# The outer product in every pair of steps from the second chunk on, and a new order of TensorE's work within a pair

## The chip, the cores and the metric

The kernel runs on one core of one Trainium2 chip. The metric is the device time of one execution in microseconds. Engines are named as the profile names them: PE is TensorE (PEld its weight loads), DVE VectorE, ACT ScalarE, POOL GpSimd, SP SyncE. ACTq and SPq are the sequencers of ACT and SP issuing DMAs.

## What is computed

A selective state space layer (two batches, 1024 steps, 512 channels, 128 states) is followed by a feed-forward layer of hidden width 2048, both with a residual and a layer norm. The recurrence is sequential in the steps and is the heart of the kernel:

```python
def step(h, inp):
    dt, bt, ct, xt = inp
    h = jnp.exp(dt[:, :, None] * A) * h + (dt * xt)[:, :, None] * bt[:, None, :]
    y = jnp.einsum('bdn,bn->bd', h, ct)
    return (h, y)
```

Its inputs come from projections of the normed input (a mask by a sigmoid, `x_proj`, softplus of `dt_proj`). Its output goes through `out_proj`, the layer norm, a gate and an up projection with silu, a down projection, and the second layer norm.

## The kernel before

**Tiling.** The 1024 steps are 8 chunks of 128 steps. The state of one batch is a tile of 128 states by 512 channels, in a ring `h` of seven steps. VectorE walks through the steps in pairs (t, t+1) with t even. For each step and batch it makes a `product` (L774, the decay `a` times the state before) and a `total` (L796, the product plus the step's input, which is `u_bc` or `v_bc` scaled by a column of `BCt`). A plain pair is eight such instructions.

**The outer product.** In a pair that is in `on_x`, the input of step t for batch 1 is not added by VectorE. TensorE adds it in PSUM instead: `add_inputs` (L1418) multiplies nine bf16 rows of `x_row` and accumulates into `m_ps[:, 1, :]`, on top of the product of (t, batch 1). VectorE's product of (t+1, batch 1), which is the one that writes `m_sb`, then reads that bank and waits for TensorE. ScalarE copies the bank into `h` (`state`, L1137), which is what the product of (t+2, batch 1) has to wait for, since it writes over the bank. Such a pair is seven VectorE instructions. The same copy must be there before `y_row` of step t.

**Who is in `on_x`.** `LOAD` gives the ScalarE time of each stage of side work in tenths of a microsecond. A running sum of it, less `X_BUDGET` (20) for each pair, must be zero. That holds for 378 of the 448 pairs from the second chunk on. The other 70 stand where softplus (`soft`), the layer norms (`ln1`, `ln2`) or squares (`sq`) fall.

**The other work of a pair.** The decays of the steps ahead are made in units q, one for each pair: POOL lays out `dexp` (L661), TensorE multiplies it with A (`exponents`, L1348, 16 matmuls of 32 rows into four banks), ScalarE takes the exponential into `a` (its `exponents`, L1120). TensorE's `exponents(q)` waits for ScalarE's of q-1, and ScalarE's for TensorE's of q. A row of the output is made from `h` and `cz` by `y_row` (L1435). All else is side work: a stage is placed by `timetable` in one of four slots of a pair (two for each step) and is carried out by TensorE and ScalarE (and POOL, for the pieces) when their loops come to that slot. All side work of TensorE goes through one PSUM bank, `work`, so that a stage waits until ScalarE has emptied it: the gate and up products `gu` (L1182, two halves for each block) are emptied by `act` (L1085 to L1089), the products `down` (L1324) by `dnc`, `outp` by `ln1`.

**The order in a pair.** Each engine carries out its instructions strictly in the order of its own loop over steps and slots. TensorE before: y rows of the two steps before, side work of slot 0, the outer product, side work of slot 1, exponents, side work of slots 2 and 3. ScalarE before: exponents, side work of slots 0, 1 and 2, `state`, side work of slot 3.

**Where it is set.** `P_AT` and `EXP_AT` map a slot to the unit q whose matmuls (TensorE) and exponential (ScalarE) are done there; slot 2t is the first slot of step t.

Of the kernel before, what the change touches and what calls it, by code (L numbers as in the profile page):

```python
# [21 lines left out]
TILES_P = KB // PAIR * BLOCKS  # L22
# [11 lines left out]
ROW = D + N  # L34
X_RING = 8
X_AHEAD = 4
X_BUDGET = 20
Z_AHEAD = 4
E_RING = 4
CZ_RING = 3  # L40
# [14 lines left out]
def exp_slot(q):  # L55


    return max(4 * q - 8 * (A_RING - 1), 2 * (q - 2))


USED_UP = {SEQ - 7: (0,), SEQ - 3: (1,)}
EXP_AT = {exp_slot(q): q for q in range(2, TILES_P)}
P_AT = {exp_slot(q) - (2 if exp_slot(q) > 2 * (q - 2) else 0): q for q in range(2, TILES_P)}
DEXP_AHEAD = 6


# [136 lines left out]
def build(nc, xT, x_rows, vecs, d_param, sel_wT, xproj_wT, dt_wT, out_wT, A_log, gu_w, down_w, out_rows):  # L203
# [5 lines left out]
    with ctx:  # L209
# [187 lines left out]
        def at_steps(t, steps):  # L397

            return [(stage, j) for step in range(max(t, 0), t + steps) for slot in (SLOTS * (step % TB), SLOTS * (step % TB) + 1)
                    for stage, _, j in plans[step // TB].get(slot, ())]  # L400
# [8 lines left out]
        on_x, busy = {}, 0  # L409
        for t in range(FIRST_X, SEQ, 2):  # L410
            busy = max(0, busy + sum(LOAD.get(stage, 0) for stage, _ in at_steps(t, 2)) - X_BUDGET)
            if not busy:
# [22 lines left out]
        def row_of(k):  # L435

            first = k % G * GP
            return x_row[first:first + RANK, k % X_RING // G, :]
# [398 lines left out]
        def scalar(e):  # L837
# [276 lines left out]
            def exponents(q, src):  # L1114
                blk = q // 2
                e.wait_ge(s_p, q + 1)
                if blk >= A_RING:
                    e.wait_ge(s_m, BATCH * BS * (blk - A_RING + 1))
                dst = a[:, blk % A_RING, :, :, q % 2 * PAIR * P:(q % 2 + 1) * PAIR * P]
                e.activation(dst.rearrange("p b t (x j) -> p x (b t) j", j=GP),  # L1120
                             src.rearrange("p g (i r j) -> p (g i) r j", i=PAIR, j=GP), ACT.Exp, scale=-1.0).then_inc(s_exp, 1)
# [26 lines left out]
            for t in range(SEQ):  # L1148
# [10 lines left out]
                for i in range(SLOTS):  # L1159
                    if SLOTS * t + i in EXP_AT:  # L1160
                        exponents(EXP_AT[SLOTS * t + i], p_ps)

# [16 lines left out]
        def tensor(e):  # L1179
# [159 lines left out]
            def exponents(q, dst):  # L1339

                if q:
                    e.wait_ge(s_exp, q)
                e.wait_ge(s_dexp, q + 1)
                for i in range(PAIR):
                    for g in range(G):
                        rows = slice(g * GP, (g + 1) * GP)
                        lays = dexp[rows, q % E_RING, BATCH * i:BATCH * (i + 1), :, :].rearrange("p b t j -> p (b t j)")
                        last = e.matmul(dst[:, g, i * COLS:(i + 1) * COLS], A[rows, q % 2 * PAIR + i, :], lays, start=True,  # L1348
                                        stop=True)
                last.then_inc(s_p, 1)  # L1350
# [61 lines left out]
            def add_inputs(t):  # L1412

                k = on_x[t]
                row = row_of(k)
                e.wait_ge(d_row[k % X_RING], 16 * (k // X_RING + 1))
                e.wait_ge(s_m, BATCH * (t + 1))
                e.matmul(m_ps[:, 1, :], row[:, D:], row[:, 0:D], start=False, stop=True, skip_group_check=True  # L1418
                         ).then_inc(s_acc, 1)

            def y_row(t):
                blk, i = t // CS, t % WIN // 2
                if t == 0:
                    e.wait_ge(s_ucp, BATCH * FIRST_U)
                elif t % WIN == 0:
                    e.wait_ge(s_ycp, t // WIN)
                e.wait_ge(s_cz, blk + 1)
                e.wait_ge(s_h, sums_before(t + 1))
                if t in on_x:
                    e.wait_ge(s_hx, on_x[t] + 1)  # L1430
                for b in range(BATCH):
                    entry = (blk % CZ_RING * BATCH + b) * CS + t % CS
                    first = GP * entry + GP - 1 - i
                    group = 2 * (t % 2) + b
                    last = e.matmul(y_ps[group * GP:(group + 1) * GP, :], cz[:, first:first + GP],  # L1435
                                    h[:, t % H_RING, b * D:(b + 1) * D], start=i == 0, stop=i == GP - 1)
                last.then_inc(s_y, 1)

            first_chunk()
            for t in range(SEQ):  # L1440
                c = t // TB
                for i in range(SLOTS):
                    if SLOTS * t + i in P_AT:
                        exponents(P_AT[SLOTS * t + i], p_ps)
                    if i == 0 and t % 2 == 0 and t:
                        y_row(t - 2)
                        y_row(t - 1)
                    if i and t in on_x:
                        add_inputs(t)
                    for stage, x, j in plans[c].get(SLOTS * (t % TB) + i, ()):  # L1450
                        behind(x, stage, j)
                        before(x, stage, j)
# [10 lines left out]
        block.vector(vector)  # L1463
        block.gpsimd(gpsimd)
        block.tensor(tensor)

# [41 lines left out]
```

## Time and profile before

| | us |
|---|---|
| Median of 3 runs | 2782.92 (2780.05 to 2787.37) |
| The profiled execution, its own time | 2790.65 |
| Its span, first to last instruction | 2788.8 |
| Busy: PE, DVE, ACT, POOL | 2432.3, 2480.8, 1735.5, 891.6 |
| Mean granted TensorE clock | 0.972 of full |

A group of rows in the profile gives line, engine, instruction, output and inputs, shape and count, then busy time, the mean of one, and the idle time of the engine just before it with what ended it. The timeline gives start, duration, engine, line, instruction and, in brackets, the idle time of the engine before it and what released it. A matmul in 32-bit floats is recorded as several passes.

### The profile page before, as it was taken

Reading aid. Unit: us, or ns where it says so; the run is one execution under the profiler, and the core shown is the slowest. Engines: PE = TensorE matmul, PEld = TensorE weight load, DVE = VectorE, ACT = ScalarE, POOL = GpSimd, SP = SyncE. Lnnn points to the kernel's source line nnn. Section 1 sums busy time; section 2 is a strip of 40 time slices with the busy share of each in tenths; the row PEclk is TensorE's granted clock in tenths of the full one; section 3 lists DMA queues with packets and bytes.
Section 4 is the critical chain, followed back from the end, with each engine's and each line's share of the span. In section 5 each row is a group of like instructions: output and inputs, shape, how many; then the busy total and the mean of one; then the engine's idle time right before and its main releaser. Section 6 shows DMA issues by size and latency. Waiting matters only on the chain.

```text
span 2788.8 us, 51274 instructions
## 1 busy us (share of the span) xinstructions
PE 2432.3 (87%) x17428; PEld 1342.1 (48%) x17428; DVE 2480.8 (89%) x3796; ACT 1735.5 (62%) x2350; POOL 891.6 (32%) x838
## 2 busy tenths in 40 slices
PE   7767679998899988989889898898989988899898
PEld 4322235554455544545445453454535545465557
DVE  6999989998998998999989889899989988988892
ACT  5555366665766666666667757667576655665653
POOL 2343323432334322342223422244223432233320
PEclk8999999999999999999999999999999999999999
DMA  5667666666666765667656675576766656777784
GB/s 168 213 213 235 215 201 199 219 209 219 199 208 209 242 227 156 206 204 248 216 170 219 205 243 195 172 224 216 229 195 199 215 192 208 222 229 236 228 274 158
DMA packets 308275, 588.00 MB, mean 211 GB/s; under 512 B 43370, under 2 KB 59956, under 8 KB 308020
## 3 DMA queue, kind: packets, MB, share of 16 engines
q1 hardware_dynamic: 251828, 449.34, 50.9%
q10 hardware_dynamic: 56192, 135.38, 14.4%
q8 instruction: 145, 2.38, 0.3%
q14 instruction: 110, 0.90, 0.1%
HBM read 565.88 MB, written 18.71 MB: 210 GB/s over the span
## 4 chain that ended last, share of the span: by engine, by line
PE 49%; DVE 19%; issue 15%; ACT 14%; DMA 2%; ACTq 1%; DVEq 0%; SPq 0%
PE banks L1182 18%; PE banks L1435 11%; DVE h L796 11%; PE banks L1348 7%; PE banks L1324 6%; ACT a L1120 5%; DVE banks L774 5%; PE banks L1418 3%; ACT L839 2%; DVE m_sb L774 1%; DVE h L794 1%; DMA U<-in_xT 1%; PE banks L1272 1%; PE banks L1276 1%; ACT L1085 1%
## 5 line engine op out<-in xcount | busy, mean ns | idle before, releaser
L774 DVE TENSOR_TENSOR banks<-a,h 128x512 f32<-128x512 f32 x1670 | 1156.6, 726 | 33.6 <-ACT h L1137 16.5
L1120 ACT ACTIVATE a<-banks 128x2048 f32<-128x2048 f32 x512 | 961.0, 1877 | 268.4 <-PE banks L1348 195.3
L661 POOL TENSOR_TENSOR dexp<-spread,dt 128x512 f32<-128x512 f32 x512 | 538.0, 1051 | 1520.6 <-DVE banks L774 1467.0
L1435 PE MATMUL banks<-h,cz 128*32 128x512 f32 x4096 | 734.1, 621 | 173.4 <-DVE h L796 147.3
L1348 PE MATMUL banks<-dexp,A 32*128 32x256 f32 x8192 | 628.5, 409 | 110.1 <-ACT a L1120 109.8
L796 DVE SCALAR_TENSOR_TENSOR h<-u_bc,BCt,banks 128x512 f32<-128x512 f32 x942 | 696.8, 740 | 0.2 <-PE banks L1435 0.2
L1137 ACT ACTIVATE h<-banks 128x512 f32<-128x512 f32 x378 | 225.9, 598 | 635.4 <-DVE m_sb L774 598.1
L1348 PEld LDWEIGHTS banks<-dexp,A 32*128 32x128 f32 x8192 | 408.0, 190 | 275.6 <-ACT a L1120 208.5
L1182 PE MATMUL banks<-vT,w_ring 128*128 128x256 f32 x1792 | 451.9, 395 | 15.7 <-ACT up L1087 15.2
L774 DVE TENSOR_TENSOR m_sb<-a,banks 128x512 f32<-128x512 f32 x378 | 258.0, 683 | 204.7 <-PE banks L1418 204.4
L1182 PEld LDWEIGHTS banks<-vT,w_ring 128*128 128x128 f32 x1792 | 325.1, 191 | 172.6 <-issue 104.7
L1435 PEld LDWEIGHTS banks<-h,cz 128*32 128x32 f32 x4096 | 126.6, 109 | 477.3 <-issue 458.3
L796 DVE SCALAR_TENSOR_TENSOR h<-v_bc,BCt,m_sb 128x512 f32<-128x512 f32 x378 | 287.9, 762 | 0.0
L1324 PE MATMUL banks<-gated,w_ring 128*128 128x256 f32 x896 | 227.8, 398 | 3.8 <-ACT vT L1092 3.8
L1324 PEld LDWEIGHTS banks<-gated,w_ring 128*128 128x128 f32 x896 | 163.9, 193 | 73.6 <-issue 49.1
L796 DVE SCALAR_TENSOR_TENSOR h<-v_bc,BCt,banks 128x512 f32<-128x512 f32 x268 | 197.7, 738 | 0.0
L1418 PE MATMUL banks<-x_row 9*128 9x512 bf16 x378 | 145.1, 384 | 15.6 <-DVE banks L774 13.8
L1418 PEld LDWEIGHTS banks<-x_row 9*128 9x128 bf16 x378 | 34.3, 91 | 255.7 <-issue 251.6
L604 POOL TENSOR_TENSOR gated<-gated,up 128x512 f32<-128x512 f32 x56 | 71.3, 1274 | 39.7 <-DVE banks L774 39.7
L601 POOL TENSOR_TENSOR gated<-gated,sg 128x512 f32<-128x512 f32 x56 | 71.2, 1272 | 36.3 <-DVE banks L774 32.5
L673 POOL TENSOR_SCALAR u_bc<-u_bc,BCt 128x512 f32<-128x512 f32 x73 | 50.7, 695 | 97.0 <-DVE banks L774 75.7
L1182 PE MATMUL banks<-U,w_sel 128*128 128x256 f32 x256 | 69.7, 422 | 8.2 <-ACT dt L869 7.1
(194 smaller groups left out, 1616.6 us busy)
## 6 DMA issues: line engine op xcount, KB each, us to landing
u_bc<-u_scratch SPq DMA_DIRECT2D x1021, 256.0 KB, 4.0
v_bc<-u_scratch SPq DMA_DIRECT2D x643, 256.0 KB, 4.0
w_ring<-in_gu_w ACTq DMA_DIRECT2D x112, 512.0 KB, 4.9
w_ring<-in_down_w ACTq DMA_DIRECT2D x56, 512.0 KB, 4.6
a<-in_gu_w ACTq DMA_DIRECT2D x16, 512.0 KB, 5.3
x_scratch<-U ACTq DMA_DIRECT2D x21, 384.0 KB, 5.7
x_row<-x_scratch SPq DMA_DIRECT2D x378, 11.2 KB
a<-in_down_w ACTq DMA_DIRECT2D x8, 512.0 KB, 4.8
```

The source lines that it names most:

```text
L601: e.tensor_tensor(pair, pair, sg[:, ring, 0:columns_of(x)], ALU.mult).then_inc(s_gm, 1)
L604: e.tensor_tensor(pair, pair, up[:, ring, 0:columns_of(x)], ALU.mult).then_inc(s_gated, 1)
L661: e.tensor_tensor(dexp[:, q % E_RING, :, :, :], spread[:, :].unsqueeze(1).unsqueeze(1).to_broadcast(shape), by_step[:, :, first:first + BS ...
L774: e.tensor_tensor(dst, a[:, blk % A_RING, b, s, :], src, ALU.mult).then_inc(s_m, 1)
L796: e.scalar_tensor_tensor(h[:, t % H_RING, part], u, BCt[c % 2][:, 0, b * TB + tl:b * TB + tl + 1], src, ALU.mult, ALU.add).then_inc(s_h, 1)
L1120: e.activation(dst.rearrange("p b t (x j) -> p x (b t) j", j=GP), src.rearrange("p g (i r j) -> p (g i) r j", i=PAIR, j=GP), ACT.Exp, scal ...
L1137: e.activation(h[:, t % H_RING, D:], m_ps[:, 1, :], ACT.Copy).then_inc(s_hx, 1)
L1182: last = e.matmul(dst, w, x, start=i == 0, stop=i == len(pairs) - 1)
L1324: last = e.matmul(dst, tile[:, sub * (HB // 4) + i, :], hidden(x, hb), start=hb == 0, stop=hb == HB - 1)
L1348: last = e.matmul(dst[:, g, i * COLS:(i + 1) * COLS], A[rows, q % 2 * PAIR + i, :], lays, start=True, stop=True)
L1418: e.matmul(m_ps[:, 1, :], row[:, D:], row[:, 0:D], start=False, stop=True, skip_group_check=True).then_inc(s_acc, 1)
L1435: last = e.matmul(y_ps[group * GP:(group + 1) * GP, :], cz[:, first:first + GP], h[:, t % H_RING, b * D:(b + 1) * D], start=i == 0, stop=i ...
```

## The change

The budget of ScalarE time goes from 20 to 100, and with that every one of the 448 pairs is in `on_x`. TensorE's exponents of unit q are done in the first slot of the even step in which ScalarE's exponential of q stood before, one step later than before; ScalarE's exponential is moved by one slot, behind the side work of slot 0. The outer product is issued in slot 0 ahead of the y rows and of all side work. TensorE's order in a pair is then: exponents, outer product, y rows, side work of slots 0 to 3. ScalarE's is: side work of slot 0, exponents, side work of slots 1 and 2, `state`, side work of slot 3. VectorE's code and POOL's are unchanged, apart from what follows from `on_x`.

```diff
-X_BUDGET = 20
+X_BUDGET = 100
...
-EXP_AT = {exp_slot(q): q for q in range(2, TILES_P)}
-P_AT = {exp_slot(q) - (2 if exp_slot(q) > 2 * (q - 2) else 0): q for q in range(2, TILES_P)}
+EXP_AT = {exp_slot(q) + (1 if exp_slot(q) > 2 * (q - 2) else 0): q for q in range(2, TILES_P)}
+P_AT = {exp_slot(q): q for q in range(2, TILES_P)}
...
                     if SLOTS * t + i in P_AT:
                         exponents(P_AT[SLOTS * t + i], p_ps)
+                    if i == 0 and t in on_x:
+                        add_inputs(t)
                     if i == 0 and t % 2 == 0 and t:
                         y_row(t - 2)
                         y_row(t - 1)
-                    if i and t in on_x:
-                        add_inputs(t)
                     for stage, x, j in plans[c].get(SLOTS * (t % TB) + i, ()):
```

## Rows read from the trace of the kernel before

**Rows 1.** The page's first part: busy time, share of the span, instructions

```profile
PE 2432.3 (87%) x17428; PEld 1342.1 (48%) x17428; DVE 2480.8 (89%) x3796; ACT 1735.5 (62%) x2350; POOL 891.6 (32%) x838
```

**Rows 2.** Waits of DVE: line and what released it, us in total, times, longest

```profile
DVE m_sb L774 <- PE banks L1418: 204.4, 164, 9.4
...
DVE banks L774 <- ACT h L1137: 16.5, 14, 3.2
```

**Rows 3.** Timeline, a pair in `on_x` without side work ahead of L1418

```profile
1002.78 1.29 DVE L774 TENSOR_TENSOR banks<-a,h 128x512 f32<-128x512 f32 x2
...
1004.53 0.38 PE L1418 MATMUL banks<-x_row 9*128 9x512 bf16 x1
1004.54 1.25 PE L1348 MATMUL banks<-dexp,A 32*128 32x256 f32 x16
...
1005.37 0.68 DVE L774 TENSOR_TENSOR m_sb<-a,banks 128x512 f32<-128x512 f32 x1
...
1006.08 0.60 ACT L1137 ACTIVATE h<-banks 128x512 f32<-128x512 f32 x1 [2.14 <-DVE m_sb L774]
...
1007.29 1.30 DVE L774 TENSOR_TENSOR banks<-a,h 128x512 f32<-128x512 f32 x2
```

**Rows 4.** Timeline, a pair with much TensorE work ahead of L1418 (step 458)

```profile
1226.94 1.06 PE L1435 MATMUL banks<-h,cz 128*32 128x512 f32 x8
...
1227.94 1.99 PE L1182 MATMUL banks<-vT,w_ring 128*128 128x256 f32 x8
...
1229.86 0.39 PE L1418 MATMUL banks<-x_row 9*128 9x512 bf16 x1
...
1230.29 0.69 DVE L774 TENSOR_TENSOR m_sb<-a,banks 128x512 f32<-128x512 f32 x1 [3.41 <-PE banks L1418]
```

**Rows 5.** By windows: the fourth chunk, and chunks two to eight (length, busy times, clock)

```profile
1027.71:1365.84 338.13, 302.11 (x2136) 165.97 (x2136) 304.28 (x462) 220.40 (x296) 110.61 (x100) 0.97 0.65 207
360.52:2725.17 2364.65, 2119.89 (x15180) 1181.23 (x15180) 2130.23 (x3218) 1530.68 (x2095) 768.81 (x704) 0.98 0.67 213
```

**Rows 6.** Timeline, three pairs of the `gu` stretch (steps 436 to 440)

```profile
1167.14 1.30 DVE L774 TENSOR_TENSOR banks<-a,h 128x512 f32<-128x512 f32 x2
...
1168.19 0.39 ACT L1085 ACTIVATE sg<-banks 128x256 f32<-128x256 f32 x1
...
1168.72 0.41 ACT L1087 ACTIVATE up<-banks 128x256 f32<-128x256 f32 x1
...
1169.12 1.00 DVE L774 TENSOR_TENSOR banks<-a,h 128x512 f32<-128x512 f32 x1
...
1171.24 1.87 ACT L1120 ACTIVATE a<-banks 128x2048 f32<-128x2048 f32 x1
...
1182.93 1.30 DVE L774 TENSOR_TENSOR banks<-a,h 128x512 f32<-128x512 f32 x2
```

**Rows 7.** Timeline of ACT: first and last instruction of a softplus

```profile
1137.40 1.28 ACT L839 ACT_TABLE_LOAD   x1
...
1141.91 0.72 ACT L912 ACTIVATE t_all<-t_all,minus_one 128x512 f32<-128x512 f32 x1
```

**Rows 8.** Timeline of ACT: first and last instruction of a layer norm

```profile
1062.86 0.60 ACT L996 ACTIVATE v<-banks 128x512 f32<-128x512 f32 x1
...
1067.16 0.72 ACT L1009 ACTIVATE v<-v,stat 128x512 f32<-128x512 f32 x1
```

**Rows 9.** Timeline of ACT: conversion and the six stores of stage `lo`, then `state`

```profile
1297.95 0.74 ACT L928 ACTIVATE U<-left 128x640 bf16<-128x640 f32 x1
...
1303.47 0.60 ACT L1137 ACTIVATE h<-banks 128x512 f32<-128x512 f32 x1 [4.78 <-DVE banks L774]
```

**Rows 10.** Timeline, step 404: `sel` on PE, and DVE waiting for `state`

```profile
1083.16 3.26 PE L1182 MATMUL banks<-U,w_sel 128*128 128x256 f32 x8 [1.19 <-ACT dt L869]
...
1083.70 0.70 DVE L774 TENSOR_TENSOR banks<-a,h 128x512 f32<-128x512 f32 x1 [0.70 <-ACT h L1137]
```

## The prediction

> **What bounds the kernel now.** I read the busy shares first, then the waits of VectorE, then the timeline pair by pair through one whole chunk. VectorE is busy 2480.8 us and TensorE 2432.3 us, ScalarE only 1735.5 us [rows 1]. So VectorE sets the pace, with TensorE close behind, and what counts is what VectorE waits for. That is almost one thing: the outer product, 204.4 us in 164 waits; waiting for `state` is 16.5 us in 14 [rows 2].
>
> A pair of seven instructions with nothing late lasts 4.51 us (1002.78 to 1007.29) [rows 3]. Call this the floor. Where POOL works beside it, VectorE's product of (t+1, batch 0) takes 1.00 us [rows 6] in place of 0.70 and the floor is 4.81 us; these are the pairs with a piece of side work on POOL, 32 of 64 in the fourth chunk by the timetable. A plain pair of eight lasts 4.98 or 5.04 us, read in the same timeline. In a pair like that of step 458 TensorE makes `gu`, y rows and `gu` again before it comes to the outer product, and VectorE stands idle 3.41 us [rows 4].
>
> The sum is made on the fourth chunk (steps 384 to 510), 338.1 us long; the seven chunks from the second on take 2364.65 us, 337.8 each [rows 5], so this chunk stands for all. Its floor is 64 x 4.51 + 32 x 0.30 = 298.2 us. The rest, 40 us, is 3.3 us for the eighth instruction in its 10 plain pairs (six of them 0.23 over 4.81, four 0.47 over 4.51), 1.5 us for two remainders that VectorE computes, and about 35 us of late outer products and what follows from them. The first chunk (plain pairs only) and the tail have no outer product, VectorE there waits for nothing that moves, and they cost nothing: TensorE's exponents run some three pairs ahead of their use.
>
> **Part 1, the outer product in 70 more pairs.** Ten a chunk. VectorE drops one instruction: minus 3.3 us a chunk. The `u_bc` scalings on POOL and v_bc loads for these pairs go too, off the path. TensorE gets ten more outer products of 0.38 us [rows 3]. ScalarE gets ten more copies of 0.60 us, and these stand exactly where ScalarE is busiest. That is the price, below in part 3.
>
> **Part 2, the new order on TensorE.** Per pair without side work, TensorE has exponents 1.1 to 1.25 us, the outer product 0.38, y rows 1.0 (1226.94 to 1227.94), and each half of `gu` or of `down` adds 1.92 us (1227.94 to 1229.86) [rows 3, 4]. The outer product can't start before the product of (t, batch 1) is done, 1.3 us into the pair; exponents put ahead of it fill just that time. If TensorE is late by x at the pair's start, the outer product starts at x + 1.1, VectorE goes on 0.42 us later (1229.86 to 1230.29 [rows 4]) and has 1.92 us to do to the pair's end (1005.37 to 1007.29 [rows 3]): the pair lasts the larger of the floor and x + 3.45. TensorE's lateness at the next pair is the side work less 0.9. So up to one half of `gu` in a pair costs nothing, where before it stood ahead of the outer product and cost up to 4 us. The long pairs of the chunk go back to 4.5 to 5.1 us (steps 390, 394, 400, 404, 458, 490: from 6.4 to 8.3). That is the gain that the 35 us hold.
>
> What the outer product costs TensorE is between 0.01 us (exponents start 0.01 after it, [rows 3]) and its own 0.38. Now the y rows, which use all 128 rows of the array, come behind it. I take 0.3, near the upper end, since nothing in 32-row pieces follows. The Trainium skill (TensorEngine Tiling (Array Packing), Key Properties) says that different row tiles can load and multiply in parallel; the start 0.01 us apart agrees. By that rule the outer product could just as well slip into the exponents ahead of it and cost nothing; this is the third rival.
>
> **What the order costs in the `gu` stretch.** Here a ring closes. Before, ScalarE's `act` followed the end of `gu` at once, since the exponential had run ahead of the pair. Now ScalarE's exponential stands ahead of `act` in slot 1 and waits for TensorE's exponents, themselves behind the last `gu`. From TensorE's start of the exponents to the next `gu`: exponents 1.2, exponential 1.77 net of overlap (1.87), `act` until the bank is empty 0.94 (1168.19 to 1169.13) [rows 6], together 3.95 us, in which TensorE has only 2.4 us of work: it idles 1.5. The ring of three pairs: 3.95 + 1.92 (`gu`) + 2.4 + 1.92 (second pair) + 2.4 + 3.84 (third) = 16.4 us, against 15.79 before (1167.14 to 1182.93 [rows 6]). Four such rings make 2.5 us a chunk, and with three more `act`s behind the exponential later, and the ends of halves that don't fit, TensorE leaves 19 us above the floor in a chunk where it and the waits behind it left 35.
>
> **Part 3, `state` behind heavy work.** VectorE's product of (t+2, batch 1) waits for the copy of t, and everything on VectorE is queued behind it, which makes TensorE's next outer product and all later steps late. ScalarE's copy normally ends 3.9 us into the pair (1006.08 + 0.60 against 1002.78) [rows 3] and is needed at 5.0. Slack: 1.1 us. Into this go a softplus of 5.2 us (1137.40 to 1142.63) [rows 7], layer norms of 5.0 (1062.86 to 1067.88) [rows 8], squares of 2.7, and a `lo` with six stores that holds ScalarE 5.5 us (1297.95 to 1303.47) [rows 9]. Where such a stage is in slot 0, the exponential follows it; the copy ends 2 to 3 us too late. In slot 1 or 2 it stands behind an exponential that begins only 1.2 us into the pair: exponential to 3.1, stage to 8.2, copy to 8.8, needed at 5.0, 3.8 us late, and more where another stage goes before. Going through the chunk in order, VectorE waits: step 384 (layer norm before) 3.0, 388 (squares) 1.0, 398 2.8, 408 (two masks and a gate) 1.1, 426 (softplus) 4.7, 456 (softplus) 2.9, 470 4.5, 488 (`lo`) 3.2, 508 4.9: 28 us. Before, most of these had no copy: the plain pairs cost 0.5 each. That such a wait is real and is not hidden is seen at step 404, 0.70 us [rows 10]. Bounds: if ScalarE had its exponential ready each time, each would be about 2 us less, 10 a chunk; the upper bound adds a slow TensorE behind each wait.
>
> **The sum.** A chunk: 298.2 floor + 1.5 + 28 + 19 = 347 us, plus 9. Seven chunks: plus 62 us. The profiled execution is 2790.65 us and would be 2853; the median of the runs shown is 7.7 lower, so 2845 us.
>
> **Rivals.** *Faster.* The waits for `state` are 10 a chunk and not 28, because TensorE and ScalarE catch up in them (a wait of VectorE gives TensorE time to finish its side work, and the following pairs start early). Then a chunk is 329, minus 9: 2720 us. The sign turns where these waits sum to 19 us a chunk. For it: 35 us of late outer products are really there [rows 2, 4]. Against it: ScalarE is strictly in order and 7.5 us of work (exponential, stage, copy) don't fit in 4.5.
>
> *Slower still.* While VectorE waits for ScalarE, TensorE has nothing that it may do, and its clock falls from 2.4 to 1.2 GHz. At step 404 the same eight passes took 3.26 us and not 1.99 [rows 10, 4], after a wait for ScalarE. With 1.3 us lost behind six of nine waits a chunk, 8 more: plus 55, 2900 us. The Trainium skill (TensorE: Matmul & The Clock Gate, What's actually happening) says that the array's clock is set by how busy it has been; by it these waits would lower the clock. The mean clock is 0.972 as it is.
>
> *No change.* The outer product costs TensorE 0.01 us and not 0.3, by slipping into the exponents: 0.3 in some 30 pairs a chunk where TensorE sets the time is 9 us, which just cancels: 2783. The opposite case, that the change doesn't do what it says, is excluded by the count: 448 copies must be there.
>
> **How the numbers follow.** Forecast (2845, between 2800 and 2875) 0.45; slower still 0.15; faster 0.28; no change 0.12. A measurement of this kernel can tell about 0.3% from no change. Of the case of no change 0.08 stays within that bound and 0.02 falls on either side, so that faster is 0.30, same 0.08, slower 0.62. The range has the faster rival's 2720 with some room and reaches to 2905: 2705 to 2905. The forecast's own range is 2800 to 2875.
>
> **What would show it.** VectorE's wait for `m_sb` from TensorE falls from 204 to about 100 us, its wait for `h` L1137 rises from 16.5 to about 190 us; L1137 counts 448 and L796 70 fewer; three pairs of the `gu` stretch take 16.4 us; TensorE waits for `up` L1087 more often; the pair of step 458 takes 4.8 us and that of step 426 some 9. I am wrong if the wait for L1137 stays under 80 us or the `gu` ring at 15.3 or less.

## The result and the profile after

The change makes the kernel slower: 2951.95 us median of 4 runs (2945.76 to 2954.2) against 2785.14 us (2780.05 to 2792.65, 4 runs), ratio 1.059 with a 95% interval of 1.0564 to 1.0619. The forecast was 2845 us with a range of 2705 to 2905. The direction was right. The size was not: plus 167 us where plus 62 were worked out.

The page's first part, engine by engine: busy time, share of the span, instructions.

```profile
span 2943.7 us, 51522 instructions
PE 2406.7 (82%) x17498; PEld 1350.3 (46%) x17498; DVE 2462.0 (84%) x3726; ACT 1771.6 (60%) x2420; POOL 868.1 (29%) x804
```

VectorE has 70 instructions fewer and ScalarE 70 more, as many as pairs were added [rows 1]. No engine has more than 84% now. What VectorE waits for (line and what released it, us in total, times, longest):

```profile
DVE banks L774 <- ACT h L1137: 267.6, 139, 5.3
DVE m_sb L774 <- PE banks L1418: 121.0, 134, 3.7
```

The waits for the outer product fell from 204.4 to 121.0 us and those for ScalarE's copy of the state rose from 16.5 to 267.6 us [rows 2]. The net is plus 168 us; VectorE's busy time fell by 18.8, and the profiled execution is 154.9 us longer (span 2943.7 against 2788.8). TensorE and ScalarE wait for each other more too:

```profile
ACT a L1120 <- PE banks L1348: 757.3, 361, 6.8
...
PE banks L1348 <- ACT a L1120: 138.6, 72, 7.2
...
ACT sg L1085 <- PE banks L1182: 91.3, 86, 4.8
PE banks L1182 <- ACT up L1087: 88.0, 52, 4.9
```

In the kernel before, ScalarE's exponential waited much less for TensorE's exponents, and TensorE's `gu` for the emptied bank:

```profile
ACT a L1120 <- PE banks L1348: 195.3, 133, 4.8
...
PE banks L1182 <- ACT up L1087: 16.0, 13, 1.5
```

The fourth chunk, which the sum was made on, and its windows row (length, busy times of PE, PEld, DVE, ACT and POOL, granted clock, DMA):

```profile
1075.91:1435.30 359.39, 298.82 (x2146) 166.33 (x2146) 301.90 (x452) 225.82 (x306) 107.93 (x96) 0.93 0.60 188
```

It was 338.1 us [rows 5], was forecast at 347, and is 359.4. TensorE's granted clock is 0.93 in it where it was 0.97. The timeline around step 426, where the softplus of step 424 ends (start, duration, engine, line, instruction, idle time before it and its releaser):

```profile
1189.93 1.28 ACT L839 ACT_TABLE_LOAD   x1
...
1190.41 0.69 DVE L774 TENSOR_TENSOR banks<-a,h 128x512 f32<-128x512 f32 x1
...
1194.43 0.72 ACT L912 ACTIVATE t_all<-t_all,minus_one 128x512 f32<-128x512 f32 x1
1195.06 0.58 ACT L1137 ACTIVATE h<-banks 128x512 f32<-128x512 f32 x1
...
1195.74 0.70 DVE L774 TENSOR_TENSOR banks<-a,h 128x512 f32<-128x512 f32 x1 [4.63 <-ACT h L1137]
...
1196.58 0.58 PE L1418 MATMUL banks<-x_row 9*128 9x512 bf16 x1 [3.55 <-DVE banks L774]
```

The copy stands behind the whole softplus (compare [rows 7]); VectorE stands still for 4.63 us, and TensorE, which waits for VectorE's product, for 3.55. This pair lasts 9.2 us. The `gu` stretch, steps 436 to 442:

```profile
1222.24 1.29 DVE L774 TENSOR_TENSOR banks<-a,h 128x512 f32<-128x512 f32 x2
...
1225.46 1.88 ACT L1120 ACTIVATE a<-banks 128x2048 f32<-128x2048 f32 x1 [3.45 <-PE banks L1348]
1227.23 0.38 ACT L1085 ACTIVATE sg<-banks 128x256 f32<-128x256 f32 x1
...
1228.21 1.99 PE L1182 MATMUL banks<-vT,w_ring 128*128 128x256 f32 x8 [1.62 <-ACT up L1087]
...
1238.28 1.29 DVE L774 TENSOR_TENSOR banks<-a,h 128x512 f32<-128x512 f32 x2
```

ScalarE waits 3.45 us for the exponents, then makes the exponential, and only then `act`; TensorE idles 1.62 us before the next `gu`. Three pairs take 16.04 us, against 15.79 [rows 6].

### The profile page after: what moved, and what is told of

Same layout as the page of the kernel before. It is cut to its first block, busy times and chain, and to the rows that moved or that the text cites. A ratio compares the mean times of both kernels' runs of the same rounds, so it can differ in the third digit from the quotient of the medians.

```text
span 2943.7 us, 51522 instructions
## 1 busy us (share of the span) xinstructions
PE 2406.7 (82%) x17498; PEld 1350.3 (46%) x17498; DVE 2462.0 (84%) x3726; ACT 1771.6 (60%) x2420; POOL 868.1 (29%) x804
## 4 chain that ended last, share of the span: by engine, by line
PE 54%; ACT 16%; issue 15%; DVE 13%; ACTq 2%; DMA 1%; DVEq 0%; SPq 0%
PE banks L1182 18%; PE banks L1348 13%; PE banks L1435 9%; DVE h L796 7%; PE banks L1324 6%; DVE banks L774 4%; ACT a L1120 3%; PE banks L1418 2%; ACT L839 2%; ACT h L1137 1%; DVE h L794 1%; PE banks L1276 1%; PE banks L1272 1%; ACT sg L1085 1%; DVE m_sb L774 1%
## 5 line engine op out<-in xcount | busy, mean ns | idle before, releaser
L774 DVE TENSOR_TENSOR banks<-a,h 128x512 f32<-128x512 f32 x1600 | 1138.5, 736 | 287.2 <-ACT h L1137 267.6
L796 DVE SCALAR_TENSOR_TENSOR h<-u_bc,BCt,banks 128x512 f32<-128x512 f32 x976 | 722.4, 740 | 0.0
L1435 PE MATMUL banks<-h,cz 128*32 128x512 f32 x4096 | 622.3, 650 | 41.2 <-DVE h L796 41.1
L1182 PEld LDWEIGHTS banks<-vT,w_ring 128*128 128x128 f32 x1792 | 343.7, 199 | 282.6 <-issue 102.2
L774 DVE TENSOR_TENSOR m_sb<-a,banks 128x512 f32<-128x512 f32 x448 | 305.5, 682 | 122.0 <-PE banks L1418 121.0
L796 DVE SCALAR_TENSOR_TENSOR h<-v_bc,BCt,m_sb 128x512 f32<-128x512 f32 x448 | 334.9, 748 | 0.0
L1137 ACT ACTIVATE h<-banks 128x512 f32<-128x512 f32 x448 | 268.1, 598 | 70.7 <-DVE m_sb L774 53.8
L1418 PE MATMUL banks<-x_row 9*128 9x512 bf16 x448 | 177.3, 396 | 144.9 <-DVE banks L774 141.4
L1435 PEld LDWEIGHTS banks<-h,cz 128*32 128x32 f32 x4096 | 89.7, 111 | 271.7 <-issue 270.2
L1418 PEld LDWEIGHTS banks<-x_row 9*128 9x128 bf16 x448 | 42.4, 95 | 204.2 <-issue 194.5
L1085 ACT ACTIVATE sg<-banks 128x256 f32<-128x256 f32 (+1 forms) x144 | 51.5, 358 | 91.4 <-PE banks L1182 91.3
L796 DVE SCALAR_TENSOR_TENSOR h<-v_bc,BCt,banks 128x512 f32<-128x512 f32 x128 | 94.7, 740 | 0.0
```

The costliest lines, as they stand in the source:

```text
L774: e.tensor_tensor(dst, a[:, blk % A_RING, b, s, :], src, ALU.mult).then_inc(s_m, 1)
L796: e.scalar_tensor_tensor(h[:, t % H_RING, part], u, BCt[c % 2][:, 0, b * TB + tl:b * TB + tl + 1], src, ALU.mult, ALU.add).then_inc(s_h, 1)
L1085: e.activation(gate, src[:, 0:cols], ACT.Tanh, scale=0.5).then_inc(s_th, 1)
L1137: e.activation(h[:, t % H_RING, D:], m_ps[:, 1, :], ACT.Copy).then_inc(s_hx, 1)
L1182: last = e.matmul(dst, w, x, start=i == 0, stop=i == len(pairs) - 1)
```

## The experiments

All ratios are to the kernel before, run on the same chip.

**The two halves of the change.** First the order alone:

```diff
 # the changed kernel
-X_BUDGET = 100
+X_BUDGET = 20
```

> The new order of TensorE and ScalarE with the old budget of 20, so that 378 pairs have the outer product. Theory A (the loss is the copies of state behind heavy ScalarE work, which come with the 70 more pairs; the order by itself is a gain): VectorE's waits for L1137 fall from 267.6 us to under 80, and the time is about 2720 us. Theory B (the order is what costs, by exponents that wait for ScalarE at the start of a pair and the gu ring of three pairs): 2850 us or more, and the ring of three pairs stays at 16.0 us. The ring should stay at 16.0 in either case.

Measured: 2854.6 us, ratio 1.024 (1.0188 to 1.0296). VectorE's waits:

```profile
DVE m_sb L774 <- PE banks L1418: 149.3, 111, 10.2
DVE banks L774 <- ACT h L1137: 120.8, 103, 3.7
```

And the budget alone:

```diff
 # the kernel before
-X_BUDGET = 20
+X_BUDGET = 100
```

> The old order with the budget of 100, so that 448 pairs have the outer product. Theory A: the waits for L1137 rise from 16.5 us to 120 or more, since heavy ScalarE work stands ahead of the copy in this order too, only that the exponential runs ahead of the pair and saves some 2 us each; about 2880 us. Theory B: 2780 us or a little less, since each of 70 pairs saves 0.47 us of VectorE.

Measured: 2901.0 us, ratio 1.0405 (1.0362 to 1.0448).

```profile
DVE m_sb L774 <- PE banks L1418: 248.3, 201, 4.3
DVE banks L774 <- ACT h L1137: 97.0, 54, 3.8
```

The order by itself costs 69 us and the budget by itself 115 us; together they would be 184, and the whole change is 167. Neither of the two theories stands alone. My expectation that the order by itself is a gain (2720 us) was wrong by 135 us. In the order alone, the waits for the copy are 103 and not the few that stand behind heavy work: an `act` between the exponential and the copy now makes the copy late, because the exponential begins late in the pair (3.2 us into the pair of step 436 above). With the budget alone, the waits for the copy are 97 us, below the 120 expected, and the waits for the outer product rise too, from 204 to 248 us. The two stand together in the longest pairs: the pair of step 470 lasts 10.7 us, with 2.91 us of waiting for the copy and then 2.76 for the outer product. Why TensorE is late behind a late copy was argued and not tested.

**The outer product early, nothing else.** In the kernel before:

```diff
                     if i == 0 and t % 2 == 0 and t:
                         y_row(t - 2)
                         y_row(t - 1)
-                    if i and t in on_x:
+                    if i == 0 and t in on_x:
                         add_inputs(t)
```

> The kernel before with one thing changed: the outer product is issued in slot 0 behind the y rows and ahead of the side work of slot 0. Exponents and exponential stay where they were. The y rows fill the 1.3 us until VectorE's product is there. If the late outer products (204 us of waits) came from side work of slot 0 ahead of it, the wait for L1418 falls to about 100 us and the time to about 2690 us. If they came from TensorE being full, whatever its order, the time stays within 0.5% of before.

Measured: 2778.6 us, ratio 0.9973 (0.995 to 0.9996). The `gu` stretch does get faster, 14.8 us for three pairs in place of 15.8, but the waits for the outer product are still 167 us:

```profile
DVE m_sb L774 <- PE banks L1418: 166.6, 117, 9.4
DVE banks L774 <- ACT h L1137: 38.4, 36, 3.7
```

The time stays within the 0.5% that the second case of the expectation named; the waits fall, but not to 100 us, and those for the copy rise from 16.5 to 38.4. Side work ahead of the outer product was worth 0.3% net. In the rest of the chunk time that is saved in one pair is partly lost in another: pair 390 goes from 7.5 to 5.8 us, pair 400 from 6.4 to 9.1.

**The exponential one slot later.** In the changed kernel, so that it stands behind the side work of slot 1 as well:

```diff
-EXP_AT = {exp_slot(q) + (1 if exp_slot(q) > 2 * (q - 2) else 0): q for q in range(2, TILES_P)}
+EXP_AT = {exp_slot(q) + (2 if exp_slot(q) > 2 * (q - 2) else 0): q for q in range(2, TILES_P)}
```

> The changed kernel with ScalarE's exponential one slot later, behind the side work of slot 1, so that act no longer stands behind it where it is in slot 1. Theory of the ring (act behind the exponential lets TensorE idle 1.5 us every third pair): the three pairs of the gu stretch fall from 16.04 to 15.4 us or less, and the copies behind act come in time; about 2920 us, since softplus and layer norms in slot 1 are then ahead of the exponential. If the ring is not what bounds this stretch, it stays at 16.0 us.

Measured: 2805.6 us, ratio 1.006 (1.004 to 1.008). It was expected at about 2920 us. This one slot is worth 146 us. The same three pairs last 14.52 us (1165.67 to 1180.19) and TensorE's next `gu` follows the y rows with no wait:

```profile
1165.67 1.29 DVE L774 TENSOR_TENSOR banks<-a,h 128x512 f32<-128x512 f32 x2
...
1168.54 1.06 PE L1435 MATMUL banks<-h,cz 128*32 128x512 f32 x8
1169.53 1.99 PE L1182 MATMUL banks<-vT,w_ring 128*128 128x256 f32 x8
...
1180.19 1.29 DVE L774 TENSOR_TENSOR banks<-a,h 128x512 f32<-128x512 f32 x2
```

So the ring through exponents, exponential, `act` and the next `gu` is what bounds that stretch, and opening it makes the three pairs shorter than the 15.4 us that I expected. The `gu` stretch is only part of the gain. In the fourth chunk, which is 25.0 us shorter (334.4 for 359.4), the eleven pairs 432 to 452 give 5.6 us; the pairs of steps 404, 458, 476, 426, 470 and 472 give 12.9 (404 falls from 8.6 to 4.5, 458 from 7.5 to 4.9). The granted clock of the whole run is 0.941 where it was 0.933.

**With the old budget too** (`EXP_AT` as above, `X_BUDGET = 20`).

> The new order with the exponential one more slot later and the old budget of 20. If the three causes simply add (late copies from the 70 pairs, act held behind the exponential, and the gain of an early outer product), this keeps only the gain: the change less its budget is 97 us faster than the change (2855 against 2952), so 2806 less about 95 gives 2710 us, faster than the kernel before by 2.5%. If the exponential's later place only gained because it made heavy ScalarE work less harmful, the two overlap and the time is about 2780.

Measured: 2730.7 us, ratio 0.9796 (0.9773 to 0.9819): faster than both kernels. The causes add in the main (2710 would be full addition, 2780 none).

```profile
DVE m_sb L774 <- PE banks L1418: 103.3, 83, 10.0
DVE banks L774 <- ACT h L1137: 51.1, 32, 3.6
```

Two variants around it. First, two slots later in place of one (`+ (3 if`):

> As the one with the exponential one slot later and the old budget, but two slots later, behind the side work of slots 0 to 2. The theory that only work that stands behind the exponential is harmed makes it equal or a few microseconds better in the gu stretch (14.5 us for three pairs); but TensorE's next exponents wait for it, and where act or heavy work is in slot 2 it ends too late: about 2730 us. If the exponential has no slack at all it is above 2780.

Measured: 2768.6 us, ratio 0.9935 (0.9914 to 0.9956). It was expected at 2730; the `gu` stretch is the same 14.5 us, and the loss is elsewhere: VectorE's waits for the outer product are 137.3 us in place of 103.3. Then a budget of 30:

> The fastest kernel so far with a budget of 30, so that 407 pairs and not 378 have the outer product. Late-copy theory: between 20 (2731 us) and 100 (2806 us) 70 pairs cost 75 us, 1.07 us for each; if the 29 pairs added at 30 are the mild ones (ScalarE's backlog running off) they cost under 10 us together, at most 2740 us; if each costs the mean, 2762 us.

Measured: 2759.5 us, ratio 0.9889 (0.9866 to 0.9913). The 29 pairs added (407 in place of 378) make it 29 us longer by the medians and 26 by the ratios, about 1.0 us each, much the same as the mean of all 70 (75 us, from 2730.7 to 2805.6). So the mild ones too lose more than they save.

**The copy ahead of the side work of slot 2.** In the changed kernel:

```diff
-                    if i and t - 1 in on_x:
+                    if not i and t - 1 in on_x:
                         state(t - 1)
```

> The changed kernel with ScalarE's copy of state one slot earlier, ahead of the side work of slot 2. Late-copy theory: the two longest pairs of the fourth chunk (steps 426 and 508, 9.2 and 9.8 us, each behind heavy work in slot 2) fall to 7.5 us or less, those behind work in slot 0 or 1 (384, 398, 456, 470) stay; VectorE's waits for L1137 fall from 268 to about 220 us and the time to about 2915 us. If something else makes these pairs long (exponents or TensorE's backlog), they stay above 9 us.

Measured: 2891.3 us, ratio 1.0374 (1.0337 to 1.041). VectorE's waits for the copy are 194.2 us in place of 267.6. Around step 426 (ACT, then DVE):

```profile
1169.64 0.61 ACT L1137 ACTIVATE h<-banks 128x512 f32<-128x512 f32 x1
1170.27 1.28 ACT L839 ACT_TABLE_LOAD   x1
```

```profile
1170.26 1.29 DVE L774 TENSOR_TENSOR banks<-a,h 128x512 f32<-128x512 f32 x2
...
1175.06 0.69 DVE L774 TENSOR_TENSOR banks<-a,h 128x512 f32<-128x512 f32 x1
```

The copy is now ahead of the softplus; pair 426 falls from 9.2 to 4.8 us and pair 508 from 9.8 to 4.5, while pair 470 (layer norm in slot 1) stays at 9.6 and 456 at 7.6. This is the late-copy mechanism, shown at its places. The time fell by more than expected (2891 for 2915), although part of the gain is lost again: VectorE's waits for the outer product rise from 121.0 to 143.4 us, and the pairs of steps 438 and 510 get longer (5.9 to 7.5 us and 5.1 to 7.6). The same edit in the fastest kernel:

> The fastest kernel so far (new order, exponential one more slot later, budget 20, 2731 us) with the copy of state one slot earlier too. With the old budget few copies stand behind heavy work, so little of the 60 us that the earlier copy gave the changed kernel is left to gain: 2715 to 2731 us. If ScalarE now idles ahead of the copy and pushes its side work of slot 2 behind it, TensorE waits for act or dnc there and it is slower, 2745 us or more.

Measured: 2726.9 us, ratio 0.9781 (0.9758 to 0.9804): this and the one without it (0.9796) can't be told apart. With the old budget there is little left for it.

**What the sum missed.** Candidates were a slow TensorE behind the waits and table loads (`ACT_TABLE_LOAD` on ScalarE ahead of some functions, 1.28 us each time) that I hadn't counted. In the edit, `heavy` gives the slot in which a pair has a softplus, a layer norm or squares. First TensorE is given matmuls that add zeros where it only waits behind heavy ScalarE work:

```diff
+            def warm(n):
+                if t % WIN < 4:
+                    return
+                for k in range(n):
+                    group = k % 4
+                    e.matmul(y_ps[group * GP:(group + 1) * GP - 1, :], cz[:, 0:GP - 1],
+                             A[:, :, :].rearrange("p k n -> p (k n)"), start=False, stop=True, skip_group_check=True)
...
+                    if i == 0 and t % 2 == 0 and t in on_x and heavy(t - 2) == 0:
+                        warm(8)
                     if SLOTS * t + i in P_AT:
                         exponents(P_AT[SLOTS * t + i], p_ps)
+                    if i == 0 and t % 2 == 0 and t in on_x and heavy(t - 2) in (1, 2, 3):
+                        warm(12)
```

> The changed kernel with extra matmuls that add zeros to the y bank (8 ahead of the exponents or 12 ahead of the outer product, 31 columns by 512) in the pair behind each softplus, layer norm or squares, where TensorE only waits; its results are unchanged. If the low clock behind these waits is what makes the loss 167 us where 62 were worked out, the granted clock rises from 0.933 towards 0.96 and the time falls by 20 to 60 us. If the low clock costs nothing there, or if TensorE's extra work is on the path, the time stays within 10 us of 2952 or is longer.

Measured: 2930.4 us, ratio 1.0515 (1.0484 to 1.0547). The clock rises from 0.933 to 0.950 and the time falls by 22 us, although TensorE does more:

```profile
PE 2475.2 (85%) x18402; PEld 1360.7 (46%) x18402; DVE 2460.4 (84%) x3726; ACT 1772.4 (61%) x2420; POOL 869.1 (30%) x804
```

Pairs 400, 428 and 472 fall from 6.2, 6.0 and 6.1 us to 4.5, 4.5 and 4.8; but pair 458 goes from 7.5 to 9.2, and its granted clock from 0.77 to 0.63. With more such matmuls, where TensorE waits for its bank:

```diff
                     for stage, x, j in plans[c].get(SLOTS * (t % TB) + i, ()):
+                        if t >= FIRST_X and (stage, j % 4) == ("gu", 0):
+                            warm(4)
+                        if t >= FIRST_X and stage == "sel" and j % 2 == 0:
+                            warm(8)
                         behind(x, stage, j)
```

> As the run with TensorE kept busy behind heavy ScalarE work (2930 us, clock 0.950), with more of the same zero-adding matmuls where TensorE waits for ScalarE to empty the bank: 4 ahead of every second block of gu, 8 ahead of sel. The low-clock theory (what is left of the missing time is TensorE running at half rate after waits) says that the clock rises to 0.965 or more and the time falls to 2890 to 2910 us. If the clock rises and the time doesn't fall, the half rate is mostly covered and something else is missing in the sum.

Measured: 2918.1 us, ratio 1.0479 (1.0446 to 1.0512), clock 0.961. Clock and time both fell short of what I expected of this run (0.965 or more, 2910 us at most). Next the table loads, in the changed kernel and in the one before:

```diff
-                    e.activation(gate, src[:, 0:cols], ACT.Tanh, scale=0.5).then_inc(s_th, 1)
+                    e.activation(gate, src[:, 0:cols], ACT.Identity, scale=0.5).then_inc(s_th, 1)
```

(and the same in the stage `gate`).

> The changed kernel with the two hyperbolic tangents of the side work replaced by a linear function of the same length, so that ScalarE doesn't have to load their table (28 loads of 1.28 us less; the sigmoids of the mask and of silu are left out by this). If these loads, which my sum left out, are a large part of what the sum missed (about 100 us), the time falls by 25 us or more and by much more than the same edit brings the kernel before. If they are covered, it falls by less than 10 us.

> The kernel before with the same edit (tangents replaced by a linear function; the sigmoids of the mask and of silu are left out): the cost of these loads in the old order. Where they stand in or behind plain pairs, as before, they should cost under 10 us: 2775 to 2785 us.

Measured: 2915.4 us in the changed kernel, ratio 1.0474 (1.044 to 1.0508), and 2766.7 us in the kernel before, ratio 0.992 (0.9891 to 0.9949). The edit, which takes 28 of 84 table loads out and with them the sigmoids of the mask and of silu, brings 37 us after and 20 us before. The loads make up the difference, 17 us of the 167 by the medians and 10 by the ratios; the intervals of the ratios are some 10 us wide to either side, so that this share is only roughly known. That they cost 20 us before was not expected either.

> The same with the tangents replaced by a linear function, so that their tables aren't loaded (the sigmoids of the mask and of silu are left out by this). If table loads and low clock are separate causes they add: 35 us below the run beside it. If the loads matter mostly because TensorE's clock falls while it waits for them, under 20 us remain.

Measured: 2888.4 us, ratio 1.0377 (1.0342 to 1.0412), clock 0.970, 30 us below the run beside it. The two causes add in the main (35 would be full addition, under 20 an overlap). Its fourth chunk:

```profile
1055.70:1402.70 347.00, 307.08 (x2362) 165.77 (x2362) 301.40 (x452) 221.59 (x304) 108.19 (x96) 0.99 0.61 195
```

Both assumptions of the sum hold in this kernel, a TensorE near its full clock and no table load for the tangents, and the chunk lasts the 347 us that were forecast.

## Why the prediction was right or wrong

**What bounds the kernel: right.** VectorE's waits decide: they rise by 168 us and its busy time falls by 18.8, which leaves 149 of the 154.9 us between the two profiled spans.

**Part 1 and part 3, the copies behind heavy work: right, place by place.** In the fourth chunk, the nine waits that were worked out one after the other came nearly as forecast (measured against forecast): 384 (4.07, 3.0), 388 (1.06, 1.0), 398 (2.80, 2.8), 408 (0.89, 1.1), 426 (4.63, 4.7), 456 (2.70, 2.9), 470 (4.68, 4.5), 488 (2.79, 3.2), 508 (5.18, 4.9). Together they are 28.8 us where the sum had 28. The waits for the copy are 268 us in all where I named "about 190". The difference is copies that the sum had not priced: eleven more in the fourth chunk, 10.0 us, most of them behind `act` and 0.9 us each. In the `gu` stretch the ring had covered them, elsewhere (404, 458, 476, 478) nothing had. Moving the copy took the two longest pairs away, shortened 384, 388 and 488 by 0.9 to 1.4 us, and left 398, 456 and 470.

**Part 2, the gain: half right.** The late outer products did go back to 121 us of waits (forecast about 100). The ring in the `gu` stretch was forecast at 16.4 us and came at 16.04, with an idle TensorE of 1.62 us where 1.5 was worked out. The 0.3 us for the outer product was somewhat too much. Exponents, outer product and y rows of step 438 on TensorE:

```profile
1230.14 1.15 PE L1348 MATMUL banks<-dexp,A 32*128 32x256 f32 x16
1231.13 0.38 PE L1418 MATMUL banks<-x_row 9*128 9x512 bf16 x1
1231.43 1.07 PE L1435 MATMUL banks<-h,cz 128*32 128x512 f32 x8
```

It starts 0.16 us before the exponents are recorded as over. From the start of the exponents to that of the y rows it is 1.29 us. Where no outer product stands between them, as here in the kernel before, it is 1.07, so the outer product costs TensorE some 0.2 us:

```profile
1054.62 1.15 PE L1348 MATMUL banks<-dexp,A 32*128 32x256 f32 x16
1055.69 1.06 PE L1435 MATMUL banks<-h,cz 128*32 128x512 f32 x8
```

The Trainium skill (TensorEngine Tiling (Array Packing), Key Properties) lets different row tiles multiply in parallel; the early start agrees with that, but the product was not free.

The ring was worked out rightly, but what I made of it was not right. I took the ring for a small loss within an order that gains. The order alone costs 69 us, and one slot of the exponential is worth 146 us in the changed kernel (124 with the old budget, 2854.6 against 2730.7), more than the budget in any order (75 to 115). The place of the exponential among ScalarE's side work is the largest single term that the runs found, and I had given it 2.5 us a chunk, with the rest of it spread over "19 us above the floor".

**The step that failed: the 19 us a chunk that TensorE was to leave above the floor.** Take from the 359.4 us of the fourth chunk the floor (298.2), the remainders (1.5) and the nine waits (28.8 measured), and 30.9 are left where the sum had 19. The pairs were summed with TensorE at its full rate and ScalarE without the table loads for the tangents, in `act` (L1085) and in the stage that empties the bank of `sel` (L869). The chunk came 12.3 us above the 347 forecast, and six pairs hold 11.7 of them (measured against worked out): 400 (6.2, 4.5), 404 (8.6, 5.1), 428 (6.0, 4.5), 458 (7.5, 4.8), 472 (6.1, 4.8), 476 (6.7, 5.7). For 400, 404 and 458, which hold 7.9, the prediction gives 4.5 to 5.1 us; the values for the other three are from the same working and are not printed in it. None of the six is among the nine places; in each TensorE is slow, or late by a table load, or both. The runs bear this out: with TensorE kept busy and the loads gone these six pairs last 31.0 us together, against 41.0 in the changed kernel and 29.4 worked out. Both faults also hang on the order, for with the exponential one slot later the six last 31.3 us, with all table loads in place. The two worst, `sel` near step 404 and `gu` in step 458, on TensorE:

```profile
1133.95 3.48 PE L1182 MATMUL banks<-U,w_sel 128*128 128x256 f32 x8 [3.13 <-ACT dt L869]
...
1283.38 3.43 PE L1182 MATMUL banks<-vT,w_ring 128*128 128x256 f32 x8 [2.64 <-ACT up L1087]
```

The windows rows around the first and of its eight passes alone (columns as above) have granted clocks of 0.84 and 0.56:

```profile
1130.00:1141.00 11.00, 7.87 (x47) 4.71 (x40) 7.08 (x12) 6.78 (x8) 2.09 (x2) 0.84 0.38 122
```

```profile
1133.95:1137.43 3.48, 3.48 (x12) 2.58 (x12) 2.05 (x3) 0.44 (x1) 0.78 (x1) 0.56 0.16 55
```

Eight passes that take 1.99 us at 2.4 GHz [rows 4] took 3.4, most of them at the lower level of 1.2 GHz, after TensorE had waited 3.13 and 2.64 us for ScalarE. "Slower still" was named as a rival with plus 55 us (2900 us) and a chance of 0.15, and it is the rival that came nearest; [rows 10] had shown its price. But the measured time is 52 us above it too, and it named the clock alone, not the table loads or the place of the exponential. The Trainium skill (TensorE: Matmul & The Clock Gate, What's actually happening) says that the clock follows how busy the array has been. The traces agree: with none, 904 and 1560 passes added in TensorE's waits the clock is 0.933, 0.950 and 0.961, and the time 2952, 2930 and 2918 us. The mean clock by itself doesn't tell the time, though: with the exponential one slot later it is 0.941 and the kernel is 146 us faster, and the two fastest kernels have 0.950 and 0.951 where the kernel before has 0.972.

**Closing the sum.** From 2845 to 2952, 107 us are missing. 14 are between the profiled executions and the medians (before 2790.65 against 2782.92, after 2945.76 against 2951.95), which the forecast carried over as minus 7.7. About 17 are table loads. 34 were recovered with TensorE kept busier; the kernel before was not run with such matmuls, so how much of the 34 the change brought in is open. Some 42 us remain by these shares. With both edits together 29 remain (2888.4 less 2845 and 14). In that kernel the second to the seventh chunk last 346.0 to 349.4 us each, close to the 347 forecast, and the last one 370 (347 in the kernel before). What makes the last chunk long was not tested. The edit to the tables helps the kernel before too (its fourth chunk falls from 338.1 to 330.7 us), so the agreement at 347 is in part luck.

**The rivals.** "Faster" needed the copies' waits under 19 us a chunk; they are 38. "No change" by a free outer product is refuted: it costs some 0.2 us, and the time is far from 2783.

## What to carry to other kernels

When two engines in strict order feed each other (exponents, exponential, bank emptied, next product), follow the round trip through both queues before moving either instruction: here one slot on ScalarE was worth 146 us and issuing the outer product ahead of the side work, alone, was worth 7. Take work off the busiest engine only where the engine that takes over its last step has room in that very stretch; each of the 70 added pairs saved VectorE 0.23 or 0.47 us, and the kernel was 1.1 to 1.6 us slower for each (75, 97 and 115 us in three orders). And when a sum says that an engine will wait, put the price of what follows the wait into it, a slower TensorE among it.

## What the runs showed of the hardware that was not expected

Keeping TensorE busy with matmuls that add nothing made the kernel faster, 22 us with 904 more passes of TensorE and 34 us with 1560. Where the clock is raised in one place, the low stretch can turn up in another (pair 458: 7.5 to 9.2 us).
